# Moving additions between VectorE, GpSimd and TensorE in an attention kernel, with small moves where its stages meet

## What is computed

```python
x = x + 0.5 * ffn(layernorm(x))
x = x + attention(layernorm(x))      # 32 heads of 32, 8 KV heads, RoPE, causal
x = x + 0.5 * ffn(layernorm(x))      # the same weights as the first
# ffn(h) = h @ base_w.T + base_b + 2 * sum_e w_e(h) * (h @ A_e.T) @ B_e.T
#          8 experts of rank 16, the two best by h @ gate_w.T, weights by softmax
```

## Time and profile before

| | |
|---|---|
| median of 3 runs | 1575.81 us (1573.46 to 1577.57) |
| profiled execution, by the clock of the runs | 1575.4 us |
| its span in the trace | 1573.6 us |
| TensorE busy (ends modelled) | 1524.4 us, 97% |
| VectorE, ScalarE, GpSimd busy | 967.3, 587.0, 694.0 us |
| mean granted TensorE clock | 0.983 |

### The profile page before, as it was taken

How to read it: one execution, slowest core, us unless ns; L and a number is a source line. 1 busy time by engine, 2 the same in 40 slices (tenths; PEclk the granted TensorE clock), 3 DMA queues, 4 the chain that set the end, 5 groups by cost and what they waited for, 6 DMA issues and landing times. The chain is left out here.

```text
span 1573.6 us, 26210 instructions
## 1 busy us (share of the span) xinstructions
PE 1524.4 (97%) x9184; PEld 1191.0 (76%) x9184; DVE 967.3 (61%) x2727; ACT 587.0 (37%) x1185; POOL 694.0 (44%) x414
## 2 busy tenths in 40 slices
PE   7999998999999969999999999999999999999999
PEld 7999998888888845555555555555478999999998
DVE  7545464556473468888888888888655434343433
ACT  4333233211111125666666666666633222121210
POOL 1222222533343415888888888888612101010100
PEclk8999999999999969999999999999999999999999
DMA  6322324342322362344433333441161212121201
GB/s 230 124 109 98 123 96 149 134 135 82 120 94 81 111 133 62 82 98 101 90 81 76 75 82 83 100 103 30 48 224 59 67 55 68 53 73 47 79 16 41
DMA packets 118774, 145.96 MB, mean 93 GB/s; under 512 B 40976, under 2 KB 77072, under 8 KB 118384
## 3 DMA queue, kind: packets, MB, share of 16 engines
q1 hardware_dynamic: 90064, 120.59, 26.5%
q10 hardware_dynamic: 28592, 23.86, 4.6%
HBM read 95.66 MB, written 53.51 MB: 95 GB/s over the span
## 5 line engine op out<-in xcount | busy, mean ns | idle before, releaser
L1504 ACT ACTIVATE at_probs<-ps 128x512 f32<-128x512 f32 (+3 forms) x768 | 324.6, 494 | 151.2 <-PE ps L1413 149.1
L1573 DVE CUSTOM_DVE_ANT_0 ps<-ps,at_score_mask 128x512 f32<-128x512 f32 (+3 forms) x512 | 290.7, 618 | 36.4 <-PE ps L1402 33.4
L329 POOL TENSOR_TENSOR f_x_ring<-f_x_ring,f_half_bias 128x1024 f32<-128x1024 f32 x32 | 77.3, 2416 | 312.8 <-DVE f_h L590 312.3
L1342 POOL TENSOR_TENSOR at_added<-at_added,at_probs 128x2048 f32<-128x2048 f32 (+1 forms) x60 | 211.4, 3523 | 2.1
L1413 PE MATMUL ps<-at_qs,at_ks 98*128 98x512 f32 (+3 forms) x528 | 192.3, 390 | 4.3 <-ACT at_probs L1504 2.9
L1402 PE MATMUL ps<-at_ks,at_qs 96*128 96x512 f32 (+3 forms) x528 | 175.4, 368 | 12.0 <-DMA at_ks<-scr_k_hi 11.3
L1413 PEld LDWEIGHTS ps<-at_qs,at_ks 98*128 98x128 f32 x528 | 97.3, 193 | 110.5 <-ACT at_probs L1504 86.4
L1428 PE MATMUL ps<-at_probs,at_vs 128*32 128x512 f32 (+3 forms) x1536 | 162.8, 496 | 0.0
L1573 DVE CUSTOM_DVE_ANT_0 ps<-ps,at_score_mask,at_part_max 128x128 f32<-128x128 f32 (+3 forms) x256 | 133.2, 556 | 12.8 <-issue 10.4
L48 PE MATMUL f_ps<-f_wt_hi,f_hT_hi 128*128 128x400 f32 (+1 forms) x384 | 134.3, 350 | 3.2 <-DVE f_hT_lo L594 3.2
L48 PE MATMUL ps<-f_wt_hi,f_hT_hi 128*128 128x400 f32 (+1 forms) x384 | 132.1, 344 | 0.0
(11 more groups left out here) (164 smaller groups left out, 3163.4 us busy)
## 6 DMA issues: line engine op xcount, KB each, us to landing
at_qs<-scr_q_hi SPq DMA_DIRECT2D x20, 512.0 KB, 5.9
f_x_ring<-in_L_attn_resid SPq DMA_DIRECT2D x16, 512.0 KB, 3.5
x<-f_x_ring SPq DMA_DIRECT2D x16, 512.0 KB, 2.7
early<-x SPq DMA_DIRECT2D x16, 512.0 KB, 3.3
scr_q_hi<-qkv_rope_hi ACTq DMA_DIRECT2D x32, 256.0 KB, 2.0
scr_q_lo<-qkv_rope_lo ACTq DMA_DIRECT2D x32, 256.0 KB, 2.3
scr_ctx<-at_ctxn SPq DMA_DIRECT2D x32, 256.0 KB, 2.3
shared<-scr_ctx SPq DMA_DIRECT2D x16, 512.0 KB, 4.5
```

Source lines behind the costliest of these rows:

```text
L329: pool.tensor_tensor(x_ring[:, u, :], x_ring[:, u, :], half_bias[:], ALU.add).then_inc(bias_added, 1)
L1342: pool.tensor_tensor(added[:, heads, :], first, probs[:, u % PROBS, heads, :], ALU.add).then_inc(added_done, 1)
L1504: act.activation(probs[:, u % PROBS, g, 0:z - a], score_ps[(u * G + g) % BANKS][:, 0:z - a], ACT.Exp, scale=SCALE).then_inc(exp_done, 1)
L1573: dve.tensor_tensor_reduce(out=src, in0=src, in1=mask, scale=1.0, scalar=part_max[:, g, own] if c else -3.0e38, op0=ALU.add, op1=ALU.max, ...
```

## The change

In the attention stage:
- `join` moves from GpSimd to VectorE, in two parts of two heads each, at u == 1 and u == 2, behind the placed row maxima and the reciprocal. TensorE waits for both parts.
- Tile 9 (384 queries) is no longer summed apart: GpSimd adds it into `added` at u == 9, behind mask 11. The division moves from u == 9 to u == 10 (the last group excepted). `added_done` counts to 6 for a group.
- In the last group VectorE adds tile 9 too, at u == 8.

At the seams:
- First FFN stage: the identity's load moves from SP's queue to ScalarE's. GpSimd adds the bias to tile 0 only when tile 0's `low_s` is there, to tile 1 when tile 1's is, and before Wq's low parts.
- Last FFN stage: GpSimd scales the bias behind tile 1's transposed low part (`hT_lo_done` 2) and no longer right behind the weights.
- QKV stage: the loads of x tiles 4 and 5 are issued ahead of weight chunk 4 and no longer behind chunk 7.

```diff
@@ ffn_stage, sync
-            if prep:
-                sp.dma_start(ident[:], consts["identity"]).then_inc(ident_loaded, 16)
             load_x(sp, 0, 0)
@@ ffn_stage, gpsimd (add_bias and low_wq hold what the loop held)
             if attn:
-                pool.wait_ge(w_lo_done, KC + 1)
+                pool.wait_ge(hT_lo_done, 2)
             pool.wait_ge(bias_loaded, 16)
             pool.tensor_scalar(half_bias[:], half_bias[:], 0.5, None, ALU.mult).then_inc(bias_ready, 1)
             pool.wait_ge(bias_ready, 1)
-            with pool.Fori(0, NT // 4, 1) as i:
+            if prep:
+                pool.wait_ge(low_ready, 1)
+            add_bias(0, 0)
+            if prep:
+                pool.wait_ge(low_ready, 2)
+            add_bias(0, 1)
+            for u in range(4):
+                if u >= 2:
+                    add_bias(0, u)
+                if prep:
+                    low_wq(0, u)
+            with pool.Fori(1, NT // 4, 1) as i:
                 for u in range(4):
+                    add_bias(i, u)
                     if prep:
+                        low_wq(i, u)
@@ ffn_stage, scalar
+            if prep:
+                act.dma_start(ident[:], consts["identity"]).then_inc(ident_loaded, 16)
             act.wait_ge(eps_set, 1)
@@ qkv_stage, sync
             for j in range(KC):
+                if j == WRAW:
+                    sp.wait_ge(h_turned, TC + 1)
+                    for slot in range(2):
+                        load_x(TC + slot, slot)
...
-            sp.wait_ge(h_turned, TC + 1)
-            with sp.Fori(TC // 2, NT // 2, 1) as i:
+            with sp.Fori(TC // 2 + 1, NT // 2, 1) as i:
@@ attention_stage
-    ADDED = range(4, 9)
-    ADDS_TO = {4: 1, 5: 1, 6: 2, 7: 3, 8: 5}
+    ADDED = range(4, 10)
+    ADDS_TO = {4: 1, 5: 1, 6: 2, 7: 3, 8: 5, 9: 6}
@@ attention_stage, gpsimd
-                    first = added[:, heads, :]
-                pool.tensor_tensor(added[:, heads, :], first, probs[:, u % PROBS, heads, :], ALU.add).then_inc(added_done, 1)
-
-            def join(n):
...
+                a, z = queries(u)
+                into = added[:, heads, a - HALF:HALF]
+                if u != ADDED[1]:
+                    first = into
+                pool.tensor_tensor(into, first, probs[:, u % PROBS, heads, 0:z - a], ALU.add).then_inc(added_done, 1)
...
-                    if u == 1:
-                        join(n)
...
-                    if u == 9:
+                    if n < NG - 1 and u == 9:
+                        add(n, 9)
+                    if u == (9 if n == NG - 1 else 10):
                         divide(n, 0)
@@ attention_stage, tensor
-                    pe.wait_ge(joined_done, n + 1)
+                    pe.wait_ge(joined_done, 2 * n + 2)
@@ attention_stage, vector
+            def join(n, heads):
+
+                dve.wait_ge(mask_done, len(diagonal) * n + (JOINED + 1))
+                dve.wait_ge(unit_done, NU * n + (NU + 1))
+                into = probs[:, 0, heads, JOINED * P:HALF]
+                dve.tensor_tensor(into, into, probs[:, JOINED, heads, 0:HALF - JOINED * P], ALU.add).then_inc(joined_done, 1)
...
+                    if u in (1, 2):
+                        join(n, slice(G // 2 * (u - 1), G // 2 * u))
-                    if n == NG - 1 and u in (4, 5, 6, 7):
+                    if n == NG - 1 and u in (4, 5, 6, 7, 8):
                         add_last(u + 1)
```

More of the change, by code:

```diff
@@ L319, in _, with add_bias, low_wq @@
             pool.sem_inc(stored[3], 16)
+            def add_bias(i, u):
+                pool.wait_ge(h_ready, 4 * i + u + 1)
+                pool.tensor_tensor(x_ring[:, u, :], x_ring[:, u, :], half_bias[:], ALU.add).then_inc(bias_added, 1)
+            def low_wq(i, u):
+                pool.wait_ge(wq_hi_done, 4 * i + (u + 1))
+                pool.tensor_tensor(wq_piece(1, i, u), wq_raw[:, u % 2, :], wq_piece(0, i, u).bitcast(F32),
+                                   ALU.subtract).then_inc(wq_lo_done, 1)
             if attn:
-                pool.wait_ge(w_lo_done, KC + 1)
+                pool.wait_ge(hT_lo_done, 2)
             pool.wait_ge(bias_loaded, 16)
@@ L324, in _ @@
             pool.wait_ge(bias_ready, 1)
-            with pool.Fori(0, NT // 4, 1) as i:
+            if prep:
[10 more added lines that the diff above has]
+            with pool.Fori(1, NT // 4, 1) as i:
                 for u in range(4):
-                    pool.wait_ge(h_ready, 4 * i + u + 1)
-                    pool.tensor_tensor(x_ring[:, u, :], x_ring[:, u, :], half_bias[:], ALU.add).then_inc(bias_added, 1)
+                    add_bias(i, u)
                     if prep:
-                        pool.wait_ge(wq_hi_done, 4 * i + (u + 1))
-                        pool.tensor_tensor(wq_piece(1, i, u), wq_raw[:, u % 2, :], wq_piece(0, i, u).bitcast(F32),
-                                           ALU.subtract).then_inc(wq_lo_done, 1)
+                        low_wq(i, u)
         @block.tensor
@@ L1597, in add_last @@
                     dve.wait_ge(last_added, u - ADDED[1])
-                    first = added[:]
-                dve.tensor_tensor(added[:], first, probs[:, u % PROBS, :, :], ALU.add).then_inc(last_added, 1)
+                    first = added[:, :, queries(u)[0] - HALF:HALF]
+                a, z = queries(u)
+                dve.tensor_tensor(added[:, :, a - HALF:HALF], first, probs[:, u % PROBS, :, 0:z - a], ALU.add).then_inc(last_added, 1)
+            def join(n, heads):
[3 more added lines that the diff above has]
+                dve.tensor_tensor(into, into, probs[:, JOINED, heads, 0:HALF - JOINED * P], ALU.add).then_inc(joined_done, 1)
             def low_ctx(t):
```

## The result

| | time, us (median, lowest to highest) | ratio to before, 95% interval |
|---|---|---|
| before | 1575.34 (1573.46 to 1577.57) | |
| changed | 1663.99 (1658.54 to 1673.64) | 1.0569 (1.0523 to 1.0614) |

Slower by 88.7 us, where +49.5 was forecast: the sign was right, and the time lies 12 us outside the range. The profiled execution of the changed kernel took 1673.64 us (span 1671.8), the slowest of its four.

The account below looks back on a forecast made before the run. TensorE was taken as the bound, with about a quarter microsecond of GpSimd slack at the second-half sum. Attention +62.8 and seams -13.3 gave +49.5 on 1575.8: 1625 us, range 1600 to 1652.

Parts of the forecast that it names:

- The bound and the place: Attention stage: TensorE's second-half sum on `added` waits some 3.3 us for GpSimd's addition of tile 9, in 15 groups.
- The freed time at unit 1: GpSimd, attention stage: removing the 3.49 us join only lengthens the wait before tile 5's addition, 0.72 to some 4.2 us.
- rival C: Chance 0.07: GpSimd's freed 3.49 us at unit 1 reach the group's end, TensorE keeps its 0.65: -24, 1552 us.
- The join: VectorE, attention stage: two join instructions of 0.84 us delay the first-half sum, +0.7 us a group, between 0 and 1.9.
- Parts 1 to 3: Attention, per steady group: tile 9 off TensorE's matmuls -0.65 us, GpSimd adding it +3.3, join on VectorE +0.7.
- Part 4: Attention stage: TensorE's granted clock falls to half behind each stall, +0.9 us per group, between 0 and 1.7.
- A: Chance 0.17, attention stage: plain stall, the clock doesn't fall and VectorE's joins hide: +39.1, with seams -13.3: 1602 us.
- B: Chance 0.18, attention stage: VectorE's joins collide with GpSimd, 1.9 instead of 0.7, clock costs 1.5: +90, seams -10: 1655 us.
- the mark that I had set for it: Attention stage: a distance between groups of 40 us and more would show B.
- D: Chance 0.06: the seam moves don't do what they say: +62.8 and about 0, 1638 us.
- The seams: Four moves on TensorE's idle times: first stage -0.4 and -4.3, QKV -4.4, last stage -4.2; together -13.3 us.
- The identity's move: First stage start: identity's DMA leaves SP's queue, so x comes up to 0.8 us earlier for VectorE: -0.4 us.

Follow-up runs that it names:

- run 3: Kernel before with only tile 9 added by GpSimd, joins kept on GpSimd and seams as before: 1657.10 us, ratio 1.0505.
- run 1: Changed kernel with tile 9 back in TensorE's sums; joins on VectorE and seam moves stay: 1578.86 us, ratio 1.0003.
- run 2: Kernel before with only the four small moves at the seams, attention stage as before: 1567.94 us, ratio 0.9935.
- run 4: Changed kernel with 13 overwritten matmuls ahead of TensorE's wait for the added tiles in 15 groups: 1620.44 us, ratio 1.0259.
- run 6: Changed kernel with 9 overwritten matmuls ahead of TensorE's wait at the second-half sum: 1617.84 us, ratio 1.0247.
- run 12: Changed kernel with the second-half sum moved behind unit 1 of the next group, whole join on VectorE: 1596.43 us, ratio 1.0119.
- run 10: Changed kernel with the second-half sum behind unit 1 of the next group, join half on VectorE, half on GpSimd: 1610.51 us, ratio 1.0205.

## Why the prediction was wrong

**What held.** The bound and the place: TensorE's sum on `added`, 15 waits, forecast 3.3 us each, measured 3.15 to 3.23 (4.07 in group 0). The freed time at unit 1 lengthened GpSimd's wait before tile 5's addition, as said, and reached nobody (rival C is out, by run 3). The join: +0.7 a group forecast, 0.73 by runs 1 and 2. Parts 1 to 3 give 34.77 + 3.3 - 0.65 + 0.7 = 38.1 us from group to group; runs 4 and 6 have 38.0 to 38.1. Without Part 4 the sum was 1575.8 + 15 x 3.35 - 1.0 - 13.3 = 1612 us, or +36, and runs 4 and 6 measured +41.6 and +39.0.

**The step that failed is Part 4, the clock.** The mechanism was right and the size wrong: 0.9 us a group, at most 1.7, against 3.1 (run 4). I took the one stretch of 3.3 us behind an idle time of 2.05 us for what every stall brings and allowed half of it as the most. But the stretch is not a fixed portion. In five of twelve cases it was 3.4 us, in one 6.8, in six 13.7 to 23.9 us, with TensorE at work all the while. A bound drawn from three single idle times at the seams was none, and a fourth in the same trace spoke against it. At the start of its attention stage the kernel before idles 11.3 us, until 563.49, and the clock then stays at half for 20 us more, most of them busy; the window, columns as above:

```profile
563.50:583.20 19.70, 17.25 (x46) 12.59 (x47) 16.51 (x65) 6.21 (x12) 1.20 (x2) 0.50 0.58 124
```

It lies inside the window of the earlier trace rows, and is most of what is missing from 1.00 in the 0.98 there. The prediction doesn't mention it. The shortfall of the forecast, 88.7 - 49.5 = 39.2 us, is 47.1 - 13.5 = 33.6 from the clock (30 by the medians alone); the rest is 2.4 from the seams and some 3 that no run divides.

**Why the stretches are so long** isn't settled. It isn't the stall's length, nor idle time of TensorE within them. Tile 9 alone has the same stall and mostly shorter stretches, 96 us in all against 140; in time the two are only 7 to 10 us apart. What the joins on VectorE add is that TensorE waits again some 12 us behind the stall, in eight groups, up to 0.6 us. All eight had a stretch of 6.8 us at most or none, and five of the six long stretches start in the group right behind one of them. That fits, but the wait wasn't tried alone.

**The rivals.** A (no clock, 1602) is wrong by the twelve stretches. B (1655) came nearest in time, for a wrong reason: its join collisions aren't there (0.95 us a join). What was said against it held: the join, right behind its transpose, comes first, and the division pays. And the mark that I had set for it, 40 us and more between groups, came out at 41.7 through the clock: a mark that two mechanisms reach tells neither. The distance at full clock would have told them apart, 38.0 against 34.77 + 3.3 - 0.65 + 1.9 = 39.3. D is out by run 2.

**The seams** brought -10.9 (run 2) against -13.3. The milestones of run 2's trace against before: first-stage routing and start -3.2 (forecast -4.7), QKV -3.0 (-4.4), attention +1.2, last stage -4.8 (-4.2). The identity's move did not do what it was made for. VectorE starts on x at 4.93 us in both traces, while the identity lands later; TensorE's first matmuls before, and in run 2:

```profile
2.64 3.67 PE L347 MATMUL f_ps<-ident 128*128 128x128 f32 x16 [2.64 <-DMA ident<-in_identity]
```

```profile
5.17 3.67 PE L362 MATMUL f_ps<-ident 128*128 128x128 f32 x16 [5.17 <-DMA ident<-in_identity]
```

The first matmul with weights follows at 12.08 us instead of 11.47: 0.6 lost where 0.4 was to be gained. The idle time of 2.05 us of the earlier trace rows is 0.43 there, and in QKV the loads of tiles 4 and 5, which the earlier trace rows has at 279.53, go out some 10 us earlier, SP's issues of run 2:

```profile
269.29 0.80 SPq L841 DMA_DIRECT2D early<-x  x2
```

The first stage's gain is not firm. In the changed kernel it is only 0.5, and over all kernels with these seams, whose first stage is the same code, one profiled execution each has from 3.9 gained (run 12) to 1.7 lost (run 10). GpSimd's bias addition, moved away from the first tile's routing, meets VectorE at a later one, in the changed kernel at 53.7 us:

```profile
53.70 2.43 DVE L630 TENSOR_SCALAR f_wf<-f_expert,f_idx_f,f_w 128x8 f32<-128x8 f32 x1
```

```profile
53.72 2.38 POOL L321 TENSOR_TENSOR f_x_ring<-f_x_ring,f_half_bias 128x1024 f32<-128x1024 f32 x1
```

```profile
58.26 0.45 PE L407 MATMUL f_ps<-ident,f_low_s 128*128 128x128 f32 x1 [3.12 <-DVE f_hT_lo L611]
```

This is the meeting of the earlier trace rows once more, 2.43 us for 8 elements a partition, and a new idle time of 3.12 us in place of the old 1.08. I had looked only at what the addition was moved away from.

## What to carry to other kernels

A wait put on TensorE's path has two prices. The first can be read from the trace to a few tenths (3.35 us a group here; runs 4 and 6 have 3.2 to 3.3); the second, the clock behind it, couldn't be bounded here from a few single idle times, and was nearly as large again where the wait came back every 40 us. Try it directly: fill the wait with matmuls that nobody reads, and see what the time does. And where work is moved from the engine at the bound to its neighbour, look who waits for the neighbour right there: 0.65 us was saved, and 3.3 waited for. Moving the wait elsewhere only passed it on, through buffer reuse, to ScalarE.

## What the runs showed of the hardware that was not expected

- More work made the kernel faster: 195 matmuls added, 44 to 47 us less (run 4), by the granted clock alone: the sum started no earlier.
- Work alone doesn't bring the clock back at once: from 673.6 to 696.4 us TensorE was busy throughout, at 0.50.
- The length of one idle time doesn't say by itself whether the clock falls. Waits of 1.05 us at the sum left it at 1.00 in every group (run 6). In the run with the sum behind unit 0 and the joins on VectorE waits of 0.9 us stood in nearly every group, and 3.4 us of half clock in ten of them. What more is in play is open.
- The instruction that pays for a meeting of VectorE and GpSimd is not always the same: a division on GpSimd (1.92 for 1.28 us), a join on VectorE (2.80 for 0.92 us), an operation on 8 elements a partition (2.43 us).
